# Sixteen-head attention of a transformer block: queries and keys transposed once and placed by DMA, with the work of four engines ordered by a model

## What is computed

```python
q = _rope(proj(Wq)); k = _rope(proj(Wk)); v = proj(Wv)     # 16 heads of 16 columns
scores = jnp.einsum('bhsd,bhtd->bhst', q, k) * attn_scale
scores = jnp.where(causal, -jnp.inf, scores)
probs = jax.nn.softmax(scores, axis=-1)
out = jnp.einsum('bhst,bhtd->bhsd', probs, v)
return out.transpose(0, 2, 1, 3).reshape(B, S, E) @ Wo.T
```

## Time and profile before

| | |
|---|---|
| Runs | 2339.97, 2342.1, 2347.78 us; median 2342.1 |
| Profiled execution | 2343.61 us; its span, first to last instruction, 2341.8 us |
| PE | busy 2037.0 us (87% of the span), 10632 matmuls |
| DVE, ACT, POOL | busy 1676.4, 1000.3 and 975.4 us |
| Second attention, projections | 1585 to 1652 us of the span |
| Second attention, heads | 1652 to 2285 us |
| Second attention, output | 2285 to 2309 us |

### The profile page before, as it was taken

The page is one execution under the profiler, slowest core; times in us unless marked ns, Lnnn a source line. Parts: engine busy times, 40 slices in busy tenths (PEclk is TensorE's granted clock), DMA queues, the critical chain, the costliest instruction groups (busy, mean ns, idle before and its releaser), DMA issues. The chain is left out here.

```text
span 2341.8 us, 36616 instructions
## 1 busy us (share of the span) xinstructions
PE 2037.0 (87%) x10632; PEld 1205.8 (51%) x10632; DVE 1676.4 (72%) x3188; ACT 1000.3 (43%) x2042; POOL 975.4 (42%) x865
## 2 busy tenths in 40 slices
PE   4757999999999999999999999567699998999996
PEld 3634555555555555555555554455454554554545
DVE  6667877878778778687787784775586785767825
ACT  1223343443434434434434434111167666666771
POOL 0023685795775856956957766013300000000000
PEclk8867999999999999999999999678799999999998
DMA  2200000000000000000000000110000000000001
GB/s 84 65 8 5 8 1 5 9 1 5 8 1 12 1 5 8 1 5 8 1 5 0 1 1 0 39 39 23 1 1 1 1 1 1 2 2 1 1 1 37
DMA packets 19790, 23.26 MB, mean 10 GB/s; under 512 B 4128, under 2 KB 17952, under 8 KB 19488
## 3 DMA queue, kind: packets, MB, share of 16 engines
q1 hardware_dynamic: 18416, 20.00, 2.8%
q10 hardware_dynamic: 1200, 1.31, 0.2%
HBM read 19.21 MB, written 2.10 MB: 9 GB/s over the span
## 5 line engine op out<-in xcount | busy, mean ns | idle before, releaser
L1100 ACT ACTIVATE lath_probs<-lath_shifted 128x512 f32<-128x512 f32 (+3 forms) x640 | 357.8, 565 | 683.3 <-DVE lath_shifted L1211 650.5
L1177 POOL TENSOR_TENSOR lath_summed<-lath_summed,lath_probs 128x512 f32<-128x512 f32 (+3 forms) x528 | 584.6, 1128 | 122.4 <-ACT lath_probs L1100 112.4
L1211 DVE TENSOR_TENSOR lath_shifted<-lath_score,lath_shift 128x512 f32<-128x512 f32 (+3 forms) x640 | 385.3, 607 | 147.8 <-PE lath_score L986 131.5
L1218 DVE TENSOR_REDUCE lath_maxima<-lath_max 128x1 f32<-128x512 f32 (+3 forms) x640 | 380.3, 605 | 132.4 <-PE lath_max L1007 84.8
L1623 DVE TENSOR_REDUCE atth_maxima<-atth_max 128x1 f32<-128x512 f32 (+3 forms) x640 | 355.1, 605 | 98.2 <-PE atth_max L1746 54.2
L1702 ACT ACTIVATE atth_probs<-atth_score 128x512 f32<-128x512 f32 (+3 forms) x640 | 313.6, 536 | 178.4 <-PE atth_score L1760 92.0
L994 PE MATMUL lath_out<-lath_probs,lat_latent 128*64 128x512 f32 (+3 forms) x1280 | 307.2, 559 | 0.0
L1007 PE MATMUL lath_max<-lat_key_hi,lath_query_hi 128*128 128x512 f32 (+3 forms) x640 | 266.0, 424 | 18.0 <-DVE lath_maxima L1218 16.5
L1746 PE MATMUL atth_max<-atth_key,atth_query 128*128 128x512 f32 (+3 forms) x640 | 267.3, 429 | 15.1 <-DVE atth_query L1595 6.2
L982 PE MATMUL lath_score<-lath_query_hi,lat_key_hi 128*128 128x512 f32 (+3 forms) x640 | 265.9, 415 | 4.0 <-DVE lath_shifted L1211 4.0
L1760 PE MATMUL atth_score<-atth_query,atth_key 128*128 128x512 f32 (+3 forms) x640 | 246.6, 407 | 14.0 <-ACT atth_probs L1702 11.6
(11 more groups left out here) (341 smaller groups left out, 2839.3 us busy)
## 6 DMA issues: line engine op xcount, KB each, us to landing
ffn_a_w<-in_L_ffn_W SPq DMA_DIRECT2D x2, 1024.0 KB, 11.7
lat_raw_out<-in_L_attn_w_out SPq DMA_DIRECT2D x8, 256.0 KB, 2.7
lat_rope<-in_c_rope_feature SPq DMA_DIRECT2D x1, 2048.0 KB, 10.8
ffn_b_w<-in_L_ffn_W SPq DMA_DIRECT2D x2, 1024.0 KB, 7.6
mix_a_factors<-in_L_ffn_factors SPq DMA_DIRECT2D x8, 256.0 KB, 4.1
out<-x SPq DMA_DIRECT2D x4, 512.0 KB, 2.9
lat_raw_q<-in_L_attn_w_q_b SPq DMA_DIRECT2D x8, 192.0 KB, 2.4
x<-in_L_attn_x ACTq DMA_DIRECT2D x2, 512.0 KB, 7.0
```

The lines of the kernel that those rows point to most:

```text
L1100: nc.scalar.activation(probs[:, prob_slot(j, kt), h, q0:CH], shifted[:, 2 * (kt % 2) + h, q0:CH], ACT.Exp, scale=SCALE0).then_inc(s["exp_d ...
L1177: last = nc.gpsimd.tensor_tensor(summed[:, j % 2, h, q0:CH], so_far, probs[:, prob_slot(j, kt), h, q0:CH], ALU.add)
L1211: nc.vector.tensor_tensor(shifted[:, 2 * (kt % 2) + h, q0:CH], score_bank[score_place(j, kt, h) % 3][:, q0:CH], shift[:, j % 2, h, q0:CH], ...
L1218: nc.vector.reduce_max(maxima[:, h, i, kc:kc + 1], max_bank[(i * (nj + 1) + kc) % 2][:, 0:width], AX.X).then_inc(s["maxima_taken"], 1)
```

## The change

The order of heads and chunks changes, and so does the way in which queries and keys get to their rows.

- In the projections POOL's rotated queries and keys go to a ring of four tiles, PE transposes each tile at once (four matmuls), ACT copies queries (`q_t`) and the keys' high part (`k_hi`), DVE makes the keys' rest (`k_lo`). SP then places every head's keys with three DMAs of 16 rows by 512 columns per head and chunk in `key`, whose rows now hold 50 per head (three parts of 16, two of ones), one head from row 0 and one from row 64. `k_hi` and `k_lo` are single: a chunk waits until the chunk before is placed.
- In the heads POOL splits the queries of eight heads at a time, SP places them with 12 DMAs per unit (four heads, one chunk), and after the shift's transpose (32 rows, one matmul) with 8 more DMAs of one row each. Nothing is transposed or copied again.
- Matmuls contract over 48 or 50 rows, from row 0 or row 64, instead of 128.
- Maxima are taken for two heads at once in slots of two banks. The diagonal blocks form one "triangle" slot with the mask added by two matmuls of 512 columns. The scores are no longer masked by PE: POOL sets the probabilities above the diagonal to zero (`affine_select`).
- The units run in the order chunk 2, 3, 1, 0, in each all four groups, unrolled. `attention_plan` simulates four engines with rough durations and writes down the order each engine follows.

```diff
+UNITS = [(c, g) for c in (2, 3, 1, 0) for g in range(NG)]
+QUERY_TILES = 4
+PROB_STEPS = 4
...
+def maxima_jobs(j):
...
+    for pair in range(2):
+        yield pair, "triangle", 0, ((0, CH),)
+        yield pair, "odd", 0, ((1, P), (3, 3 * P))
+        yield pair, "even", 0, ((2, 2 * P),)
+        for i in range(TPC):
+            for kc in range(j):
+                yield pair, "whole", kc, ((i, CH),)
...
+def attention_plan():
...
+    query_ready = {n: 8.0 + 2.5 * n for n in range(QUERY_TILES)}
...
+            ready_at[n] = vector_at + 4.0
...
-        attention_projections(core, qk, v, w_o_t)
-        attention_heads(core, qk, v, attended)
+        attention_projections(core, q_t, key, v_one, w_o_t, attended)
+        attention_heads(core, q_t, key, v_one, attended)
...
+                for h in range(H1):
+                    sp.dma_start(key[head_rows(h, PLACED, 2), h // 2, :].bitcast(F32).rearrange("p (a b) -> p a b", b=P),
+                                 core.ones[0:2, :].unsqueeze(1).broadcast_to([2, NT, P])).then_inc(s["ones_placed"], 16)
+                for c in range(NCH):
+                    cols = slice(c * CH, (c + 1) * CH)
+                    sp.wait_ge(s["k_high_done"], 2 * c + 2)
+                    sp.wait_ge(s["k_low_done"], 2 * c + 2)
+                    for h in range(H1):
+                        half, rows = h // 8, slice(D1 * (h % 8), D1 * (h % 8) + D1)
+                        for part, of in enumerate((k_hi, k_lo, k_hi)):
+                            sp.dma_start(key[head_rows(h, D1 * part, D1), h // 2, cols].bitcast(F32), of[rows, half, :].bitcast(F32)).then_inc(s["keys_placed"], 16)
...
+                    if t % TPC == 2 and c >= 0:
+                        act.wait_ge(s["turned_back"], TPC * (c + 1))
+                        for half in range(2):
+                            if c >= 1:
+                                act.wait_ge(s["keys_placed"], 16 * 3 * H1 * c)
+                            nc.scalar.activation(k_hi[:, half, :], bank[2 + half][:], ACT.Copy).then_inc(s["k_high_done"], 1)
+                        for half in range(2):
+                            nc.scalar.activation(q_t[:, half, c * CH:(c + 1) * CH], bank[half][:], ACT.Copy).then_inc(s["q_taken"], 1)
...
+                        for f in range(4):
+                            last = nc.tensor.transpose(bank[f][:, i * P:(i + 1) * P], turned[:, back % 4, f * P:(f + 1) * P], core.ident)
+                        last.then_inc(s["turned_back"], 1)
...
+                def place_queries(n):
+                    m, g = n // 2, UNITS[n][1]
+                    if n >= QUERY_TILES:
+                        sp.wait_ge(s["scores_done"], GROUP * (last_step[n - QUERY_TILES] + 1))
...
+                for n in range(QUERY_TILES):
+                    place_queries(n)
+                for e in plan["vector"]:
+                    if e[0] == "turn":
+                        n = e[1]
+                        sp.wait_ge(s["slot_taken"], reads[e[2]])
...
+                        for h in range(GROUP):
+                            for c in range(2):
+                                rows = slice(TPC * (2 * h + c), TPC * (2 * h + c) + TPC)
+                                sp.dma_start(query[head_rows(h, PLACED + c, 1), n % QUERY_TILES, h // 2, :].bitcast(F32)
+                                             .rearrange("o (i q) -> o i q", q=P), shift_t[rows, n % 2, :].bitcast(F32)).then_inc(shift_placed[n % 2], 16)
+                        if n >= 1 and n - 1 + QUERY_TILES < len(UNITS):
+                            place_queries(n - 1 + QUERY_TILES)
...
+                        if kt == 0 and h == 0:
+                            pe.wait_ge(shift_placed[n % 2], per_shift * (n // 2 + 1))
+                        if u >= 3:
+                            pe.wait_ge(s["exp_done"], u - 2)
+                        q0 = queries_from(kt, j)
+                        nc.tensor.matmul(score_bank[u % 3][:, q0:CH], key_rows(GROUP * g + h, PLACED + 2, kt * P, P),
+                                         query_rows(n, h, PLACED + 2, q0, CH - q0), start=True, stop=True).then_inc(s["scores_done"], 1)
```

More of the change, by code:

```diff
@@ L1429, in attention_schedule @@
-def attention_schedule(first, last):
-    placed = []
-    for step, j, together in placed_events():
-        if step >= 0 and not (first and j < 0):
-            placed += together
-        elif step < 0 and not last:
-            placed += [(at + KT_PER_PAIR, in_chunk(event, j, j + NCH)) for at, event in together]
-    placed.sort(key=lambda e: e[0])
-    events = []
-    for j in range(NCH):
-        for kt in range(key_tiles(j)):
-            follow = (j, kt - LAG) if kt >= LAG else (j - 1, key_tiles((j - 1) % NCH) - LAG + kt)
-            atoms = [[("scores", j, kt, 0)], [("scores", j, kt, 1)], [("scores", j, kt, 2)], [("scores", j, kt, 3)], []]
-            if not (first and j == 0 and kt < LAG):
-                atoms[4] += [("values", *follow, half) for half in range(2)]
-                if kt == LAG - 1:
-                    atoms[4].append(("drain", j - 1))
-            for n, atom in enumerate(atoms):
-                events += atom
-                while placed and placed[0][0] < STEPS_BEFORE[j] + kt + (n + 1) / len(atoms):
-                    events.append(placed.pop(0)[1])
-    return events + [event for _, event in placed]
@@ new lines, in attention_projections, with attention_heads @@
+    core.end_step()
+def attention_heads(core, q_t, key, v_one, attended):
+    nc = core.nc
+    plan = attention_plan()
+    ring = {e[2]: e for e in plan["tensor"] if e[0] in ("maxima", "turn", "finish")}
+    place = {(e[0], e[1]): e[2] for e in plan["tensor"] if e[0] in ("turn", "finish")}
+    last_step, masked_before = {}, {}
+    for e in plan["scalar"]:
+        if e[0] == "scores":
+            last_step[e[1]] = e[4]
+    for k, e in enumerate(plan["pool"]):
+        masked_before[e[3]] = k
+    reads, taken = {}, 0
+    for e in plan["vector"]:
+        if e[0] in ("maxima", "turn", "finish"):
+            j = UNITS[e[1]][0]
+            taken += len(MAXIMA[j][e[3]][3]) if e[0] == "maxima" else 2 if e[0] == "finish" else 1
+            reads[e[2]] = taken
@@ L1588, in place @@
-        def place(engine, group, what, copy):
-            kind, j, pair, n, local = what
-            wait(engine, s["side_done"], side_use(group, local) + 1)
-            if kind == "turn_keys":
-                copy(key[:, pair, (j % NCH) * CH:(j % NCH + 1) * CH], side_bank[:]).then_inc(s["side_free"], 2)
-            else:
-                copy(query[rows_of(n), j % NCH, 2 * pair + n, :], side_bank[rows_of(n), :]).then_inc(s["side_free"], 1)
-        with nc.Block() as block:
+        queries_placed = [core.sem(f"atth_queries_placed{i}") for i in range(2)]
```

691 lines of the change are left out of this document (360 added, 331 removed).

## The result

The changed kernel takes 2354.1 us, median of 8 runs (2350.9 to 2367.7), the kernel before 2341.1 us (2339.2 to 2347.8): a ratio of 1.0056, 95% interval 1.0040 to 1.0073. It is slower by 0.56%, where 2245 us and "faster" at 0.84 were forecast; it also lies above the range. The profiled execution takes 2350.85 us, its span is 2349.0, so it misses the forecast by 106 us: the change was to save 4% and saves nothing.

The account below looks back on a forecast made before the run. PE was taken as the bound, losing some time to both partners. From a span of 2341.8 us, heads 442 instead of 633 and projections +92.5 gave 2243.3, plus 1.8 around the span: 2245 us, range 2180 to 2335.

Parts of the forecast that it names:

- the issue as the price, whatever the size: Projections: each key placement DMA costs SP 0.495 us of issue, 24 us per chunk; the part grows by 92.5 us.
- PE's demand, 347 us: Heads: PE's work falls to 347 us from 523: scores 82, maxima 114, values 140, shift turns and finishes 11.
- 0.27: Heads: us taken per wide pair of matmuls, two heads in two halves of the rows.
- The rival of the changed shape: Heads: each change of the array's shape costs 0.16 us, 53 us in all, total 2298; chance 0.10.
- my 0.15 us around a values group: Heads: overhead counted for each values group, besides 0.85 us for its four float32 passes at 512 columns.
- The trace's only changes, around values, leave 0.15 us for both: Heads: argument on the shape rival: both shape changes around a values group together cost 0.15 us.
- Heads, start, 43 us: Start of the heads: scores begin at +43 us, after the whole first unit's maxima, shift, copy and placement.
- Late shifts, 15 us: Heads: shifts placed later than planned stop PE, 0 to 42 us over 15 units; a third, 15 us, taken.
- PE is used for 0.87 of the stretch. That share is what mutual waiting leaves, and I keep it.: Heads: PE's share of use, 523 of 602 us before, kept for the changed kernel.
- a clock that falls in the heads: Heads: named only under anything else, with two rivals together as another example; chance 0.02 for all of it.
- 384 for 334: Heads after the start: PE's remaining 334 us of work at a use of 0.87 take 384 us.
- a placement DMA costs what the longest issue costs: Projections rival: the long DMA issue adds 200 us, total 2353, slower; chance 0.04.

Follow-up runs that it names:

- e2: Changed kernel with keys placed in two rounds of 48 DMAs of 1024 columns instead of four of 512: 2325.5 us, ratio to before 0.9915.
- e8: Kernel without the computation, only PE prices at length: alternating halves 0.114 us apart, eight halves and a values group 2.14 us.
- e5: Changed kernel with each shift placed by four DMAs of two rows instead of eight of one: 2316.3 us, ratio to before 0.9893.
- e11: e10 with measured times for queries and shifts in the engine model that makes the order: 2271.0 us, ratio to before 0.9681.
- e10: Changed kernel with e2 and e5 together, order unchanged: 2280.9 us, ratio to before 0.9729.
- e4: Changed kernel plus 12 extra matmuls on half the rows before each unit's wait for its shift: 2374.2 us, ratio to before 1.0125.
- e9: As e4, but the extra matmuls use all 128 rows (identity times mask, bf16): 2348.9 us, ratio to before 1.0012.
- e1: Kernel without the computation, only PE and SP prices: DMA issues 0.45 us apart from HBM, 0.63 to 1.02 us from SBUF.
- e6: Changed kernel with 84 of the 160 values groups using 256 of 512 columns: 2361.6 us, ratio to before 1.0060.
- e7: Changed kernel with reduces of maxima other than the triangles reading half their columns: 2350.5 us, ratio to before 1.0030.

## Why the prediction was wrong

- **Projections, "the issue as the price, whatever the size", 0.495 us.** The structure was right (SP bounds, back to back, ACT, POOL and DVE wait) and e2 confirms it. The price came from loads from HBM; a placement inside SBUF costs 0.63. 192 x 0.135 = 26 us more; the first started 6 us earlier than I said, and the gaps were 3.4 instead of 4.5 us. Together +16 us: 1760 instead of 1744.
- **Heads, PE's demand, 347 us.** About right. With e8's prices: scores 224 x 0.23 + 96 x 0.2 = 71; maxima 192 x 0.23, 32 triangles of 1.03 and 19 for the narrow, 96; values 112 x (0.915 + 0.30) and 43 for the narrower, 179; turns and finishes 11: 357 us. Pairs were cheaper than 0.27, values dearer than 1.00 us. The rival of the changed shape was right in its mechanism, 0.15 us per change, but my 0.15 us around a values group had taken half of it. "The trace's only changes, around values, leave 0.15 us for both" was misread from the earlier trace rows: with the neighbours' starts they leave some 0.3, and the kernel before pays them too. By the rule of the Trainium skill (TensorEngine Tiling, Key Properties: changing the tiling mode drains TensorE) that cost was to be expected, and e8 agrees with 0.15 us.
- **Heads, start, 43 us.** First exponential 49 us after the part's begin: 20 DMAs in its way at 0.63 instead of 0.5 us, and DVE's 23 us as said. +6.
- **Late shifts, 15 us.** The stops were 18 us, nine of them. The step failed in taking the stop as the whole price: e5 gains 38.
- **"PE is used for 0.87 of the stretch. That share is what mutual waiting leaves, and I keep it."** This is the step that failed. The share came from a stretch at a granted clock of 0.96. In the changed kernel the clock of 1820 to 2292 is 0.85, and 0.62 in chunk 0 (2243 to 2292), where DVE and ACT have little and PE stands twice for a placement, 4.9 us. Of the nine stops for a shift five are followed within 3 us by a stretch at 0.50, of 7 to 14 us; at three the clock was low already, and behind one it stayed at 1.00. Five other stretches at 0.50 have no late shift at their start. Of "a clock that falls in the heads" I had spoken in the rest, with 0.02 together.
- **The account of the 81 us missed in the heads.** In the profiled execution 532 - 49 - 18 = 465 us remain for a demand of 344 (forecast: 384 for 334). In e11 three units of chunk 3 have a clock of 1.00 throughout and take 43.5 us in the mean (42.4 to 44.9) for 35 us of demand, 0.80 to 0.81; at that share 344 would take 427. So about 12 us are demand, 31 the share at the full clock, and some 38 go with the clock. That last number is what is left over. A second estimate comes from pairs of runs with the same order on PE, between the first exponential and the last values: e2 has 22 us more at half the clock than the changed kernel and takes 7 us longer, e10 15 more than e5 and 5 longer, e4 69 more than e9 and 17 longer beyond its extra matmuls. That is 0.25 to 0.31 us lost per us at half the clock, and the changed kernel has 153 us of it: 38 to 47 us.
- **The 0.87 was also read too low.** With 1.2 instead of 1.00 us per values group, an estimate, PE's demand in the kernel before was 555 us of 602, 0.92. The too low price stood in both sums: 344 / 0.92 would have given 374 us, near the 384 of the forecast, so this error was hidden by its twin. Measured the same way the changed kernel uses PE for 344 of 465 us, 0.74 instead of 0.92.
- **Why less work keeps the clock low.** Before, PE had 523 us of work in 602 (555 by the prices of e8 and e1) and the clock held. Now it has 357 in 532, much of it on 48 or 50 rows. The halves together keep 1.00 when fed without a gap (e8), one half alone does not; e6 shows that taking work from PE lowers the clock further, and e9 that whole-array work put into the stops raises it (0.82 to 0.90 over 1774 to 2292). The Trainium skill (TensorE: Matmul & The Clock Gate, Part 1: The HAM clock gate) ties the clock to how busy PE has been, and e8 adds that busy time alone does not keep it. A rule I should have weighed: by it the change, which takes a third of PE's work away, puts its clock at risk.
- The other rivals: "a placement DMA costs what the longest issue costs" fell (0.63, not 1.02); DVE is no bound of the units (e7).

Left open: what the heads would take at a full clock throughout. No kernel here reached it (best 0.94, in e9, from the first exponential to the last values), and nothing was tried that keeps PE busy inside the units. Nor is it settled why e6 gained nothing.

## What to carry to other kernels

Taking a third of the matmul work from PE can lower its granted clock and give part of the time back: price PE's remaining work at the clock that the thinner stretch will get, and a late transfer as its stop plus the slow stretch that can follow it. To price a group of matmuls, read the starts of its neighbours as well as its own. Where DMAs inside SBUF replace transposes, count the DMAs: 0.63 us of issue each up to 16x1024, so fewer and wider ones win (29 us for the keys, 38 for the shifts). A fixed order made by a model is worth tens of us either way, so its rare long times must be measured ones, and an order that collects work of one kind can empty the buffers of its partner (three banks here; no run varied their number).

## What the hardware showed that I had not expected

- PE busy without a gap on 50 rows of one half falls to 1.2 GHz (granted clock 0.50, 0.43 us between starts of 512 columns instead of 0.23); alternating halves stay at 2.4 GHz and start 0.114 us apart (e8).
- Two matmuls of the same half in a row cost 0.11 us more than alternating ones, a change between halves and strips 0.15 us (e8), one between the whole array and strips 0.14 us (e1).
- A us at half the clock cost the heads 0.25 to 0.31 us here, an estimate from pairs of runs with the same order.
- A DMA's issue on SP costs 0.45 us from HBM; from SBUF 0.63 us with 16 rows of 512 or 1024 columns, 0.73 us with 128 rows of 512 and 1.02 us with 16 rows of 2048 (e1, e2).
